# AdaLN-style conv and grouped FFN in two layers: output kept by rows, x1 gathered and added before the scatter, x1's turned tiles stored from ScalarE's queue

## The reference

```python
# layer 0: per-sample 1x1 conv, then linear + mixed LoRA, residual
x = x + ffn0(cond0(x, cond_128, ...), W, bias, A, Bf, coeffs, scales)
# layer 1
c = conv1d(x, weight, 9 taps, groups=4) + (cond_128 @ c_weight.T)[:, :, None] + fside   # [32,128,2048]
t = c.reshape(4096, 2048)[:, perm].reshape(4096, 16, 128)
t = gelu(einsum('bhd,hdm->bhm', t, up))          # 16 heads, 128 -> 512
t = einsum('bhm,hmd->bhd', t, down)              # 512 -> 128
x = x + t.reshape(4096, 2048)[:, argsort(perm)].reshape(32, 128, 2048)
```

## Time and profile before

| | us |
|---|---|
| median of 3 runs | 2507.34 (2507.33 to 2508.14) |
| the profiled execution | 2513.49 |
| its span, first to last instruction | 2511.7 |
| PE busy | 2432.4 (97%) |
| DVE busy | 1713.9 (68%) |
| ACT busy | 1113.7 (44%) |
| POOL busy | 938.1 (37%) |

### The profile page before, as it was taken

The page is one execution under the profiler, slowest core; times in us unless marked ns, Lnnn a source line. Parts: engine busy times, 40 slices in busy tenths (PEclk is TensorE's granted clock), DMA queues, the critical chain, the costliest instruction groups (busy, mean ns, idle before and its releaser), DMA issues.

```text
span 2511.7 us, 37065 instructions
## 1 busy us (share of the span) xinstructions
PE 2432.4 (97%) x11130; PEld 2010.9 (80%) x11130; DVE 1713.9 (68%) x2449; ACT 1113.7 (44%) x1850; POOL 938.1 (37%) x826
## 2 busy tenths in 40 slices
PE   8899999999999999999999988999999999999985
PEld 6788888888888888887888866888888888888864
DVE  6665555875555855558544665778888888888865
ACT  3221211321212322223222356777777777777753
POOL 2275654556645255323233311222222222222331
PEclk9999999999999999999999999999999999999988
DMA  8965554755543767657555665468888888888898
GB/s 301 326 214 187 199 174 159 258 177 205 202 163 132 269 219 225 204 178 258 178 172 172 194 196 153 141 189 244 242 245 248 240 240 243 245 246 245 231 245 255
DMA packets 397563, 540.90 MB, mean 215 GB/s; under 512 B 37016, under 2 KB 262640, under 8 KB 397360
## 3 DMA queue, kind: packets, MB, share of 16 engines
q1 hardware_dynamic: 295872, 309.50, 43.0%
q10 hardware_dynamic: 77376, 152.17, 16.2%
q0 software_dynamic: 24112, 76.80, 9.9%
HBM read 309.72 MB, written 228.61 MB: 214 GB/s over the span
## 4 chain that ended last, share of the span: by engine, by line
PE 88%; DMA 5%; DVE 3%; issue 2%; SPq 1%; ACT 1%; POOL 0%; ACTq 0%; DVEq 0%; POOLq 0%
PE ps_c L463 45%; PE ps_up L1401 13%; PE ps_y L1411 13%; PE ps_c L1426 9%; PE ps_v L441 4%; PE ps_c L429 3%; DMA u_s<-z_d,idx 1%; DVE w_lo L1006 1%; PE ps_up L1426 1%; SPq L88 1%; DMA rear<-x_d 1%; DVE ring_lo L953 1%; DMA w_hi<-y_d 1%; DMA x_n<-in_up 0%; DVE x_s L1002 0%
## 5 line engine op out<-in xcount | busy, mean ns | idle before, releaser
L463 PE MATMUL ps_c<-w_hi,ring_hi 128*128 128x512 f32 x1792 | 703.9, 393 | 4.9 <-DVE r_early L1002 3.6
L463 PE MATMUL ps_c<-w_hi,ring_lo 128*128 128x512 f32 x1792 | 698.0, 390 | 0.0
L463 PE MATMUL ps_c<-w_lo,ring_hi 128*128 128x512 f32 x1792 | 697.9, 389 | 0.0
L613 ACT ACTIVATE ring_hi<-raw_n 128x512 fp32r<-128x512 f32 x382 | 239.6, 631 | 852.2 <-DVE raw_n L944 232.1
L1581 DVE TENSOR_TENSOR g_lo<-kern,g_hi 128x512 fp32r<-128x512 f32 x512 | 349.2, 687 | 80.3 <-ACT g_hi L1483 71.3
L463 PEld LDWEIGHTS ps_c<-w_hi,ring_hi 128*128 128x128 f32 x1792 | 336.8, 188 | 75.8 <-DVE ring_lo L953 4.7
L463 PEld LDWEIGHTS ps_c<-w_hi,ring_lo 128*128 128x128 f32 x1792 | 336.5, 188 | 69.8
L463 PEld LDWEIGHTS ps_c<-w_lo,ring_hi 128*128 128x128 f32 x1792 | 336.8, 188 | 67.5
L1383 POOL DMA_INDIRECT y_d<-y_room,idx x128 | 131.8, 1030 | 651.7 <-ACT y_room L1516 584.9
L1002 DVE TENSOR_TENSOR r_early<-ps_c,r_early 128x512 f32<-128x512 f32 x256 | 176.4, 689 | 275.9 <-PE ps_c L463 275.9
L1479 ACT ACTIVATE kern<-ps_up 128x512 f32<-128x512 f32 x512 | 304.5, 596 | 118.4 <-PE ps_up L1401 102.8
(11 more groups left out here) (188 smaller groups left out, 3628.0 us busy)
## 6 DMA issues: line engine op xcount, KB each, us to landing
u_d<-raw_n ACTq DMA_DIRECT2D x64, 512.0 KB, 3.2
x_d<-r_early ACTq DMA_DIRECT2D x128, 256.0 KB, 3.5
raw_n<-u_d SPq DMA_DIRECT2D x64, 512.0 KB, 3.6
x_d<-x_s ACTq DMA_DIRECT2D x126, 256.0 KB, 2.8
u_s<-x_d SPq DMA_DIRECT2D x496, 64.0 KB, 2.4
z_d<-x_s SPq DMA_DIRECT2D x120, 256.0 KB, 4.7
rear<-y_d SPq DMA_DIRECT2D x224, 128.0 KB, 3.7
rear<-x_d SPq DMA_DIRECT2D x56, 512.0 KB, 4.4
```

The source lines that it names most:

```text
L463: mm = nc.tensor.matmul(bank, a[:, dc, :], w[k][:, dc, :], start=(first and dc == 0 and n == 0), stop=(dc == 3 and n == 2), skip_group_che ...
L613: nc.scalar.activation(ring_hi[g % RING][:].rearrange("p a n -> p (a n)"), factor(q, k, p), ACT.Copy).then_inc(hi_ready, 1)
```

## The change

Three things change in layer 1. The output leaves the kernel as rows (`out` is [8·2048, 512]; the host turns it back), so a step's result is added to x1's gathered rows and scattered straight to `out`; the way back through `y_d` and the end phase go. For this x1 itself must lie in rows: DVE also transposes each unit of x1 (`turn_x`), and each tile of four units is stored to a new `xt_d`, from ACT's queue. POOL gathers its rows (`gather_row`) beside those of z. And the loop is written out.

ScalarE loses the copy of y and gets the stores of x1's tiles, its own step being:

```diff
-                    nc.scalar.activation(y_s[j], ps_y[j][:, 0, :], ACT.Copy).then_inc(y_ready, 1)
...
+            def step(u, s):
+                if s >= 0 and s + 2 < STEPS:
+                    split_t(s + 2)
+                if s < 0:
+                    split_x(u + 1)
...
+                if u < STEPS:
+                    take_z(u)
+                if u == H - 1:
+                    act.wait_ge(zt_ready, H)
+                    store_tile(act, z_d, z_tiles, z_out, G - 1, range(2, S))
+                if s >= 0 and u + 1 < STEPS:
+                    split_x(u + 1)
+                if u < STEPS and u % SB == SB - 1:
+                    tile = u // SB
...
+                    act.wait_ge(xt_ready, u + 1)
+                    store_tile(act, xt_d, x_tiles, xt_out, tile, range(S))
+                if s < 0 <= s + 2:
+                    split_t(s + 2)
...
+                for mc in range(MC):
+                    if 0 <= s + 1 < STEPS:
+                        gelu(s + 1, mc)
```

What is shared by both kinds of tile, and the casts of ScalarE (three of four, not two):

```diff
+        def tile_of(tiles, tile):
+            return tiles[tile % 2 if tile < G else 0]
+
+        def last_tile_user(tile):
+            return tile - 2 if tile <= G else tile - 1
+
+        def tile_free(eng, stored, tile):
+
+            last = last_tile_user(tile)
+            if last >= 0:
+                eng.wait_ge(stored[last % 2], 64 * (last // 2 + 1))
...
-            return mc % 2 == 0
...
+            return mc != 1
...
+        def store_tile(eng, dram, tiles, stored, tile, quarters):
+            for r in quarters:
+                eng.dma_start(sh.turned_rows(dram[tile // G % 2], r, tile % G),
+                              tile_of(tiles, tile)[r * GC:(r + 1) * GC].rearrange("p w b c -> p w (b c)")).then_inc(stored[tile % 2], 16)
```

SyncE's loads of x1 now also wait for `turn_x` of the unit that had the buffer (u - 4 for u < H + 2, else u - 2), and its stores of z come behind them:

```diff
+            def load_rows(u):
+                _, b, g = place(u)
+                last = last_xp_user(u)
+                wait(sp, xlo_ready, last + 1)
+                wait(sp, xt_ready, last + 1)
+                if u == 3:
+                    sp.wait_ge(sh.item_mm, LAST)
...
+            def step(u, s):
+                if u + 4 < H + 2:
+                    load_rows(u + 4)
+                elif H <= u and u + 2 < STEPS:
+                    load_rows(u + 2)
+                if u < STEPS and u % SB == SB - 1:
...
+                    sp.wait_ge(zt_ready, u + 1)
+                    store_tile(sp, z_d, z_tiles, z_out, tile, range(2 if tile == G - 1 else S))
```

GpSimd's step, and VectorE's new functions and step:

```diff
+                if 0 <= s + AHEAD < STEPS:
+                    gather_t(s + AHEAD)
+                if 0 <= s + 2 < STEPS:
+                    gather_row(s + 2)
+                if s >= 0:
+                    scatter(s)
...
+            def turn_x(u):
+                tile = u // SB
+                if u % SB == 0:
+                    tile_free(dve, xt_out, tile)
+                nc.vector.transpose(tile_of(x_tiles, tile)[:, :, u % SB, :],
+                                    xp[xp_of(u)][:, 1:Q + 1].rearrange("p (w c) -> p w c", w=WIDE)).then_inc(xt_ready, 1)
...
+            def add_rows(s):
+                dve.wait_ge(down_done, MC * (s + 1))
+                dve.wait_ge(row_in[s % 2], 16 * (s // 2 + 1))
+                nc.vector.tensor_tensor(rows[:, s % 4, :], ps_y[s % 2][:, 0, :], rows[:, s % 4, :], ALU.add).then_inc(o_ready, 1)
...
+                if s < 0:
+                    split_x(u + 1)
...
+                    turn_z(u)
+                    turn_x(u)
+                    if 0 <= s + 2:
+                        split_t(s + 2)
+                else:
+                    if u < STEPS:
+                        turn_x(u)
+                    if s + 2 < STEPS:
+                        split_t(s + 2)
+                    if u < STEPS:
+                        turn_z(u)
+                    if u + 1 < STEPS:
+                        split_x(u + 1)
+                for mc in range(MC):
+                    if 0 <= s + 1 < STEPS:
+                        split_g(s + 1, mc)
+                    if s >= 0 and mc == MC - 2:
+                        add_rows(s)
```

More of the change, by code:

```diff
@@ L1053, in _, with layer1_block @@
             take(LAST - 1)
-def layer1_block(nc, block, sh, x1_d, up, down, perm, ident, z_d, y_d, out):
+def layer1_block(nc, block, sh, x1_d, up, down, perm, z_d, xt_d, out):
     with ExitStack() as ctx:
@@ L1077, in layer1_block @@
[L1077 to L1085, removed]
@@ L1086, in layer1_block @@
[L1086 to L1094 removed]
+        x_turned = sb("x_turned", [P, 4 * Q])
+        rows = sb("rows", [P, 4, RB])
@@ L1130, in layer1_block @@
[L1130 to L1154, removed]
@@ L1228, in z_rows, with chunks_of, place @@
-        def z_rows(dram, r, part):
-            return dram.rearrange("(w i r) n -> r i w n", w=WIDE, r=S)[r, :, :, part * C:(part + 1) * C]
-        def before(k, h, n=1):
-            return (k, h - n) if h >= n else (k - 1, h - n + H)
-        def after(k, h):
-            return (k, h + 1) if h < H - 1 else (k + 1, 0)
+        def chunks_of(u):
+            n = EARLY + 2 * (u - 4)
+            return range(n, n + 2) if EARLY <= n < CHUNKS else ()
+        def place(u):
+            tile = u // SB
+            return tile, SB * (tile // G) + u % SB, tile % G
@@ L1239, in _, with drive @@
+        def drive(step):
+            for u in range(LEAD + STEPS):
+                step(u, u - LEAD)
         @block.sync
         def _(sp):
[L1241 to L1248 removed]
+            sp.dma_start(idx[:, 0, :], perm).then_inc(small_in, 16)
+            def load_rows(u):
[5 more added lines that the diff above has]
+                    sp.wait_ge(sh.item_mm, LAST)
+                if u == H:
@@ L1336, in _ @@
+            load_rows(3)
+            sh.store_last()
+            drive(step)
         @block.gpsimd
@@ L1626, in build @@
     z_d = [scratch(f"z_d{j}", [L, RB]) for j in range(2)]
-    y_d = [scratch(f"y_d{j}", [L, RB]) for j in range(2)]
+    xt_d = [scratch(f"xt_d{j}", [L, RB]) for j in range(2)]
     with ExitStack() as ctx:
@@ L1632, in build @@
                      conv_w, ctx_w, fside, ident, up, down, aggb_d, aggw_d, weff_d, t_d, u_d, x1_d)
-        layer1_block(nc, block, sh, x1_d, up, down, perm, ident, z_d, y_d, out)
+        layer1_block(nc, block, sh, x1_d, up, down, perm, z_d, xt_d, out)
 def kernel(**inputs):
```

474 lines of the change are left out of this document (152 added, 322 removed).

## The result

The changed kernel takes 2634.49 us (median of four runs, 2625.27 to 2638.27) where the kernel before takes 2507.34: ratio 1.0503, 95% interval 1.0475 to 1.0531. The forecast was 2590, slower. The profiled execution took 2633.84 us, its span is 2632.0.

A forecast was written before the change was run, and what follows sets the result against it. PE's own 33 matmuls were taken to bound a full step. End -49, lead-in +33, gaps +65 and clock +34 sum to +83 us, 2590 us on the median's scale; range 2505 to 2640 us.

The forecast's parts named there:

- The end, -49: Behind layer 1's last convs: idle PE and lost clock go (-20.8 us), and what follows the last scatter goes (-27).
- DVE, ACT and POOL in a full step, nothing: Layer 1's full steps: DVE's work about even, ACT's cast and POOL's third indirect DMA cost 0 us, hidden by PE.
- The lead-in, +33: Start of layer 1, where SP's issuing sets the pace: four added items sum to +34 us, taken as +33, bounds +15 and +50.
- chain of loads behind `turn_x`: Lead-in: loads wait for `turn_x`, 7 us a unit where SP's queue took 2.8; three units, +12 us.
- Term (c): Lead-in: the fifth tile's stores stand on ACT before `split_t(1)` and the first gelus, +4 us.
- (b): Lead-in: each of the first three tiles adds 5.8 us of shared store time, 5 taken for each, +15 us.
- (d): Lead-in: unit 3's load waits for layer 0's end and unit 4's for x1's first transpose, +3 us.
- z's tile free at T+16.3, so 2.5 us of gap and +65: Full steps, T the start of a tile's last conv: `turn_z` must start by T+13.8, so PE waits in 26 tiles.
- the head start of 0.9 us: Full steps: ACT can begin x's stores at T+2.8, 0.9 us before z's stores began at T+3.7; subtracted from z's free time.
- The clock, +34: Full steps: clock lost behind each of 26 PE gaps, 1.3 us each, bounds 0 and 3.2 us each.
- Queues side by side: Rival 1, full steps: SP's and ACT's stores served together, z free at T+11.4, nothing waits; -27 us, 2480 us, chance 0.12.
- ACT as the bound: Rival 3, full steps: ACT held until both tiles' stores are through, PE waits on `g_lo`; +47 us, 2637 us, chance 0.1.

The follow-up runs named there:

- the run with both further moves: On x one step earlier, x1 turned 3.5 us sooner except a tile's first unit, and both tile-opening turns moved to mid-step on DVE: 2478.53 us, ratio 0.9889.
- x one step earlier: Changed kernel with `turn_x(u + 1)` done in step u and, from the fifth tile, x's tile stored from SP the step before z's: 2509.24 us, ratio 1.0018.
- the run with few pieces: Changed kernel with each of x's four stores writing 32 runs of 8 KB instead of 512 pieces of 512 bytes: 2595.46 us, ratio 1.0355.
- the run with the moved turn: Changed kernel with `turn_z` in each tile's first step placed behind `add_rows`, not ahead of the split of x1: 2500.11 us, ratio 0.9977.

## Why the prediction was right, and what it had wrong

The direction, the place and the chain were as forecast; the time came 44 us above the forecast and inside its range. Between the profiled executions the change is +120 where +83 was forecast; these 37 us are the gaps (21), the clock (15), the end (5), less the lead-in (1) and layer 0 (3). The rest is the distance of the two executions from their medians, 6.15 and -0.65 us. By its own steps:

- *The end, -49.* Measured -17.2 in the stretch behind the last convs and -26.5 in the end phase, so -44. Two gaps of PE stayed in the first (1.42 and 0.78 us).
- *DVE, ACT and POOL in a full step, nothing.* Right, and shown: the run with both further moves has full steps of 809.8 us, as before, with all of that work in them.
- *The lead-in, +33.* Measured +32.1. Its largest term, the chain of loads behind `turn_x`, is there in the trace, three splits 6.0 to 6.4 us apart (x one step earlier took 20.4 us of the 32 off, though that run moved the stores too). Term (c), the fifth tile's stores, had 4 us and looks too small: without them the lead-in is 8.5 us shorter. (b) and (d) were not measured apart.
- *z's tile free at T+16.3, so 2.5 us of gap and +65.* The due time held: T+13.8 asked, T+17.9 got, is 4.1, and that tile's gap was 3.99; on the mean of the 26 tiles it is T+17.3 and 3.3 us, +86. The free time was 1.0 us too early, and the term that was mis-sized is the head start of 0.9 us. The loads stand between x's stores and z's on SP, are issued later than before because they wait for `turn_x`, and are held, so z's stores begin at T+6.8 and not at T+3.7. The same sum without the head start gives 11.4 + 5.8 = T+17.2. But it isn't z's late start that costs: started at T+4.1, the tile was free at T+17.3 on the mean again. The 5.8 us for four more stores were right in size, and the reason I gave, "a store of 512 pieces occupies something that both queues share for 1.45 us", only in half: shared is right, the pieces are not. With a sixteenth of the pieces x's stores still held ACT for 3.64 us and brought z's tile only 1.0 us sooner. What fits all of these runs is the time of the 16 DMA engines themselves: x's and z's stores, the loads and the gathers make one burst of 3.9 MB that keeps them at a share of 0.93 to 1.11 from T+6 to T+18. I didn't measure that limit by itself; that it isn't mainly the count of pieces, nor z's place in SP's queue, nor ACT's hold is shown.
- *The clock, +34.* Measured +49, 1.9 us a tile where I took 1.3, inside the bounds of 0 and 3.2. The price was too low, and not because the gaps came out longer: in the run with few pieces the 26 gaps are 2.4 us each, about as long as I had forecast, 62 us in all, and the full steps grew by 111, so 49 are left there too.
- *Rivals.* Queues side by side: no; the full steps are 944.8 us with x's stores on ACT's queue and 813.7 without them. ACT as the bound: no; PE's gaps are released by `xp_lo`, and the run with the moved turn keeps ACT's hold of 4.1 us at full steps of 812.1.

What I didn't see at all is that the late transfer costs only by what stands behind the wait for it. I worked out what is queued behind `turn_z` on DVE (the split, 0.65 us, then all `g_lo`) as a term of the sum, and took the queue as given. It was the cheapest thing in the kernel to change.

## What to carry to other kernels

When a wait appears, ask first what stands behind the waiting instruction on its engine and whether it has to: moving one transpose behind the work that the critical engine needs gave back 134 us, with the transfers as late as they were. Of the attempts on the transfers, storing x a whole step earlier gave back 125 us, 104 of them in the full steps, and x's transposes 3.5 us earlier on top of that gave nearly all of the rest; three that left x's stores beside z's or put them behind (all from one queue, z's ahead of the loads, x's one step later) made things worse. Two single-buffered tiles whose stores fall into the same step make a burst that a mean DMA share of 0.61 doesn't show, below the 0.80 of the kernel before; take the share in windows as short as the deadline, and compare how long it stays near 1 with the same place before. Before issuing big stores ahead of small loads, look up when the loads are due: in the two runs that did so the loads came late; in the one on the changed kernel the stores were through no sooner.

## What the runs showed of the hardware that was not expected

The issue of a DMA from SP or ACT is held while stores of either queue are under way (SP's loads for up to 1.61 us each), and ACT's hold is nearly the same for 32 runs of 8 KB as for 512 pieces of 512 bytes (3.64 and 4.21 us for four stores of 256 KB). Loads of 64 KB issued behind four such stores landed late enough for ACT to idle 8.36 us. And a gap of PE of 3.3 us on the mean, once in 36 us, cost more than half of its own length again by the clock: 49 us for 86 us of gaps. The clock's part hardly follows the length of the gaps: by the same subtraction it is 1.9 us a gap for gaps of 2.4 us (few pieces), 1.9 for 3.3, 2.1 for 5.7 (all stores from SP) and 2.4 for 6.8 (z's stores ahead of the loads on the changed kernel); the lowest is 1.6 for 2.7 (the same on x one step earlier). With gaps of 1.9 us and less (x one step earlier) PEclk of the full steps is 1.00.
